# Edge scatter of a fused graph-network kernel: four one-hot buffers of four chunks in place of two, edge bias in PSUM banks of its own, first one-hots between the evictions of the values

## The reference

```python
x = x + L0_gnn(layernorm(x), batch, edges, edge_attr_16, Wq, ..., 32)   # 512 nodes, 512 wide, 8 heads
x = x + L0_ffn(layernorm(x))                                            # 8 experts, top 2
x = x + L1_gnn(layernorm(x), edges, edge_weight, ...)                   # Chebyshev, 5 terms
x = x + L1_ffn(layernorm(x))                                            # 8 experts, top 2

# L0_gnn, 32 graphs of 16 nodes
attn = einsum('bnhd,bmhd->bnmh', q, k) * scale
eb = edge_attr @ We + be                       # 16384 edges, 8 heads
attn = attn.at[src // n, src % n, dst % n].add(eb)
attn = softmax(attn, axis=2)
out = einsum('bnmh,bmhd->bnhd', attn, v)

# L1_gnn
deg = segment_sum(edge_weight, src)
norm_w = -dinv[src] * edge_weight * dinv[dst]
prop(h) = segment_sum(norm_w[:, None] * h[src], dst)
```

## Time and profile before

| | |
|---|---|
| time, median of 3 runs | 792.26 us (791.27 to 792.68) |
| time of the profiled execution | 792.48 us |
| its span | 790.7 us |
| PE, DVE, ACT busy, share of the span | 86%, 71%, 56% |
| first triple of the scatter starts, closing matmuls start | 66.96 us, 162.94 us |
| PE's granted clock, mean over the span | 0.932 |

### The profile page before, as it was taken

One profiled execution on the slowest core, in us unless ns is written; L12 is line 12 of the kernel. 1 busy time (PEld: TensorE's weight loads), 2 busy tenths in 40 slices (PEclk: granted clock), 3 DMA queues, 4 the chain that ended last, 5 costly groups with the idle time before them and its releaser, 6 DMA issues.

```text
span 790.7 us, 23111 instructions
## 1 busy us (share of the span) xinstructions
PE 676.8 (86%) x8392; PEld 569.0 (72%) x8393; DVE 563.3 (71%) x1237; ACT 444.2 (56%) x772; POOL 119.8 (15%) x175
## 2 busy tenths in 40 slices
PE   2997999957488999999993499999399999999991
PEld 1456888844378999999983244444288999999981
DVE  4665777653779888898887473435778888887881
ACT  3452666632256777787765332220367888788870
POOL 2000000010000022323214100000000234233333
PEclk9998999979679999999997699999579999999996
DMA  9500110110126889989863830000137889988864
GB/s 305 221 1 3 41 40 0 40 41 1 71 90 241 320 277 338 308 256 325 284 217 68 313 107 1 1 0 1 70 110 239 257 259 271 268 266 262 259 200 86
DMA packets 37779, 127.72 MB, mean 162 GB/s; under 512 B 5441, under 2 KB 6033, under 8 KB 37569
## 3 DMA queue, kind: packets, MB, share of 16 engines
q1 hardware_dynamic: 31712, 119.39, 43.5%
q0 software_dynamic: 3648, 6.23, 5.4%
q10 hardware_dynamic: 2352, 1.23, 0.6%
HBM read 117.85 MB, written 10.03 MB: 162 GB/s over the span
## 4 chain that ended last, share of the span: by engine, by line
PE 64%; DVE 16%; issue 7%; DMA 5%; ACT 3%; POOL 2%; ACTq 1%; DVEq 1%; SPq 0%; POOLq 0%
PE pb L1479 11%; PE pb L1480 11%; PE pb L1481 11%; PE pb L1718 6%; PE pb L1580 5%; DMA r_stage<-in_chunks 4%; PE pb L1749 3%; PE pb L1751 3%; PE pb L1750 3%; DVE r_split L950 3%; PE pb L1578 2%; PE pb L1488 2%; ACT r_split L679 2%; PE pb L1579 1%; DVE r_work L1263 1%
## 5 line engine op out<-in xcount | busy, mean ns | idle before, releaser
L950 DVE SCALAR_TENSOR_TENSOR r_split<-r_stage,r_split 128x1024 f16<-128x1024 f32 (+1 forms) x160 | 230.7, 1443 | 48.8 <-ACT r_split L679 47.1
L679 ACT ACTIVATE r_split<-r_stage 128x1024 f16<-128x1024 f32 (+1 forms) x160 | 197.2, 1236 | 49.4 <-PE pb L1751 32.3
L1479 PE MATMUL pb<-r_work,r_split 128*128 128x160 f16 x864 | 185.1, 235 | 6.8 <-DVE r_work L1339 5.1
L1480 PE MATMUL pb<-r_work,r_split 128*128 128x160 f16 x864 | 185.1, 235 | 0.0
L1481 PE MATMUL pb<-r_work,r_split 128*128 128x160 f16 x864 | 185.0, 235 | 0.0
L1749 PE MATMUL pb<-r_work,r_split 128*128 128x160 f16 x608 | 129.9, 233 | 5.4 <-DVE r_work L1327 2.8
L1751 PE MATMUL pb<-r_work,r_split 128*128 128x160 f16 x608 | 129.9, 233 | 0.0
L1750 PE MATMUL pb<-r_work,r_split 128*128 128x160 f16 x608 | 129.9, 233 | 0.0
L1578 PE MATMUL pb<-r_work 128*128 128x64 f16 x512 | 88.3, 195 | 5.2 <-DVE r_work L1075 3.0
L1479 PEld LDWEIGHTS pb<-r_work,r_split 128*128 128x128 f16 x864 | 85.3, 99 | 8.6 <-issue 6.9
L1580 PE MATMUL pb<-r_work 128*128 128x256 f16 x512 | 90.6, 277 | 0.0
(11 more groups left out here) (284 smaller groups left out, 1289.0 us busy)
## 6 DMA issues: line engine op xcount, KB each, us to landing
r_stage<-in_chunks SPq DMA_DIRECT2D x68, 768.0 KB, 4.5
r_stage<-in_chunks SPq DMA_DIRECT2D x92, 512.0 KB, 4.9
r_gnn<-in_cheb_lin SPq DMA_DIRECT2D x3, 1024.0 KB, 8.6
r_split<-in_cheb_lin SPq DMA_DIRECT2D x3, 1024.0 KB, 11.6
x_dram<-x_sb SPq DMA_DIRECT2D x10, 256.0 KB, 2.6
x_sb<-in_x SPq DMA_DIRECT2D x1, 1024.0 KB, 5.7
r_split<-in_Wq SPq DMA_DIRECT2D x1, 1024.0 KB, 9.5
r_work<-in_attr SPq DMA_DIRECT2D x1, 1024.0 KB, 11.2
```

The lines of the kernel that those rows point to most:

```text
L679: nc.scalar.activation(x.hi(c), x.stage(c), ACT.Copy, scale=W_SCALE).then_inc(x.whi, 1)
L950: V.scalar_tensor_tensor(x.lo(c), x.stage(c), W_SCALE, x.hi(c), ALU.mult, ALU.subtract)\
L1479: MM(o, sh, mh, start=start, stop=False)
L1480: MM(o, sh, ml, start=False, stop=False)
```

## The change

- **Four buffers.** In the narrow path there are four buffers (`NB` = 4) of four chunks, 7 KB a partition each (`dst` now holds 64 columns a chunk and no longer 512). DVE and ACT wait for the use of a buffer three buffers back.
- **Sources.** ACT makes one source one-hot of four in every buffer (two of eight, where it was three of eight); DVE makes the other three. ACT reads `flag_i` too, as its path now depends on it.
- **Edge bias** accumulates in `pb[6]` and `pb[7]`. PE waits for `v_ready` only before it opens the accumulations, and no longer for `score_read`. `score_m` moves to another place in SBUF.
- **Order on DVE.** One-hots of buffer 0, evictions of v 0 and 1, buffer 1, evictions 2 and 3, buffer 2, the scores, buffer 3. Within a buffer the edge-bias products now come ahead of the two weight products. `weight_lo` is done after each eight buffers, as before.
- **PE** reads `flag_i` before the v projection. Its loop body is eight rounds of two buffers (two iterations), where it was four rounds (four iterations). The closing matmuls have one column each.

The diff, cut to its core:

```diff
-        score_m = [view(r_work, 8 + b, T * H // 2 * GN, F32, "p (t h k) -> p t h k", t=T, h=H // 2) for b in range(2)]
+        score_m = [view(r_mid, 12 + b, T * H // 2 * GN, F32, "p (t h k) -> p t h k", t=T, h=H // 2) for b in range(2)]
+        NB = 4
+        src_hot_n = [view(r_work, 7 * b, GC * N, F16, "p (c n) -> p c n", c=GC) for b in range(NB)]
+        dst_n = [[view(r_work, 7 * b + 4 + 0.5 * s, GC * W, F16, "p (c n) -> p c n", c=GC) for s in range(2)]
+                 for b in range(NB)]
+        ebd_n = [view(r_work, 7 * b + 5, GC * 2 * P, F16, "p (c s q) -> p c s q", c=GC, s=2) for b in range(NB)]
...
-            def sources(i, b, free):
+            def source(b, one, hot, n):
+
+                nc.scalar.activation(src_off[:, b % 2, :], iota_n[:, :], ACT.Abs, bias=src_neg[:, one])\
+                    .then_inc(off_ready, 1)
+                act.wait_ge(off_ready, n)
+                nc.scalar.activation(hot, src_off[:, b % 2, :], ACT.Relu, bias=ones[:, 0:1], scale=-1.0)\
+                    .then_inc(hot_act, 1)
+            def sources(i, b, bufs, hot, free):
-                    act.wait_ge(hot_used, i * 2 + (b - 1))
-                if free or b > 0:
-                    act.wait_ge(hot_act, i * (2 * AC - 1) + b * AC)
-                for c in range(AC - b):
-                    one = bass.ds(i * (2 * GC) + (b * GC + c), 1)
+                    act.wait_ge(hot_used, i * bufs + (b - bufs + 1))
+                if free or b >= 2:
+                    act.wait_ge(hot_act, i * bufs + (b - 1))
+                source(b, bass.ds(i * (bufs * GC) + b * GC, 1), hot[b][:, 0, :], i * bufs + (b + 1))
...
+            narrow = act.value_load(flag_i[0:1, 0:1], min_val=0, max_val=1)
+            with act.If(narrow):
+                all_sources(NB, src_hot_n)
+            with act.Else():
+                all_sources(2, src_hot)
...
-            for t in range(T):
+            def take_scores():
-            def one_hots(i, b, free, windowed):
+            def targets(b, at, hot, ebd_b, windowed):
+
+                for c in range(1, GC):
+                    V.tensor_scalar(hot[:, c, :], iota_n[:, :], src_f[:, at(c, 1)], None, ALU.is_equal)
+                for s in range(2):
+                    last = V.tensor_tensor(ebd_b[:, :, s, :].rearrange("p c (h m two) -> p c h m two", h=H, two=2),
+                                           bc(pairs(dl_hot[:, at(0, GC), :]), 2, H),
+                                           bc(eb_2[s][:, at(0, GC), :, :], 3, GN // 2), ALU.mult)
+                return last
+
+            def near_hots(i, b, free):
+
+
+                def at(c, n):
+                    return bass.ds(i * (NB * GC) + (b * GC + c), n)
+
+                if free:
+                    dve.wait_ge(hot_used, i * NB + (b - NB + 1))
+                V.tensor_tensor(pairs(rel_hot[b % 2]),
+                                bc(iota_n[:, 0:W].rearrange("p (m two) -> p m two", two=2), 1, GC),
+                                bc(rel_2[:, at(0, GC), :], 2, W // 2), ALU.is_equal).then_inc(rel_ready, 1)
+                targets(b, at, src_hot_n[b], ebd_n[b], True)
+                dve.wait_ge(rel_ready, i * NB + (b + 1))
+                for s in range(2):
+                    last = V.tensor_tensor(pairs(dst_n[b][s]), pairs(rel_hot[b % 2]),
+                                           bc(w_2[s][:, at(0, GC), :], 2, W // 2), ALU.mult)
+                last.then_inc(hot_ready, 1)
...
-            def all_one_hots(windowed):
-                rounds = C // (2 * GC) // AHEAD
+            def all_near():
+                near_hots(0, 0, False)
+                values(0)
+                values(1)
+                near_hots(0, 1, False)
+                values(2)
+                values(3)
+                near_hots(0, 2, False)
+                take_scores()
+                near_hots(0, 3, False)
+                rounds = C // (NB * GC)
                 for c in range(AHEAD):
-                    if c == 0:
-                        one_hots(0, 0, False, windowed)
-                        one_hots(0, 1, False, windowed)
-                    with dve.Fori(max(1, rounds * c), rounds * (c + 1)) as i:
-                        one_hots(i, 0, True, windowed)
-                        one_hots(i, 1, True, windowed)
+                    with dve.Fori(max(1, rounds // AHEAD * c), rounds // AHEAD * (c + 1)) as i:
+                        for b in range(NB):
+                            near_hots(i, b, True)
                     weight_lo(ex[0], 0, c)
...
-            dve.wait_ge(score_read, 2 * T)
...
-                        pb[4 + i][:, :].rearrange("p (t s q) -> p t s q", t=2, s=2)[:, :, s, :],
+                        pb[6 + i][:, :].rearrange("p (t s q) -> p t s q", t=2, s=2)[:, :, s, :],
...
+            narrow = pe.value_load(flag_i[0:1, 0:1], min_val=0, max_val=1)
...
-            def scatter(i, b, windowed, firsts, after=None):
-                pe.wait_ge(hot_ready, i * 2 + (b + 1))
-                pe.wait_ge(hot_act, i * (2 * AC - 1) + (AC + b * (AC - 1)))
+            def scatter(i, b, bufs, c0, hot, hi, lo, ebd_b, firsts=None, after=None):
+                pe.wait_ge(hot_ready, i * bufs + (b + 1))
+                pe.wait_ge(hot_act, i * bufs + (b + 1))
...
-                        last = MM(pb[4 + t // 2][:, 256 * (t % 2):256 * (t % 2) + 256], w,
-                                  ebd[b][:, c, :, :].rearrange("p s q -> p (s q)"), start=False, stop=False,
+                        w = hot[:, c, t * P:(t + 1) * P]
+                        MM(pb[t][:, cols], w, hi[:, c, 0:n], start=False, stop=False, skip_group_check=True)
+                        MM(pb[t][:, cols], w, lo[:, c, 0:n], start=False, stop=False, skip_group_check=True)
+                        last = MM(pb[6 + t // 2][:, 256 * (t % 2):256 * (t % 2) + 256], w,
+                                  ebd_b[:, c, :, :].rearrange("p s q -> p (s q)"), start=False, stop=False,
...
-                turns = 4
+                turns = 8
                 with pe.Fori(0, C // (2 * GC * turns)) as i:
                     firsts = window_starts(i * (2 * GC * turns))
...
-                        scatter(i * turns + r, 0, True, firsts)
-                        scatter(i * turns + r, 1, True, firsts, load_next if r < turns - 1 else None)
+                        for h in range(2):
+                            b = (2 * r + h) % NB
+                            scatter(i, 2 * r + h, 2 * turns, h * GC, src_hot_n[b], dst_n[b][0], dst_n[b][1], ebd_n[b],
+                                    firsts, load_next if h == 1 and r < turns - 1 else None)
...
             pe.wait_ge(v_ready, T)
-            pe.wait_ge(score_read, 2 * T)
-            for t in range(T + 2):
-                MM(pb[t][:, :], zeros[:, :], iota_n[:, :], start=True, stop=False, skip_group_check=True)
-            narrow = pe.value_load(flag_i[0:1, 0:1], min_val=0, max_val=1)
+            totals = [pb[t] for t in range(T)] + [pb[6], pb[7]]
+            for o in totals:
+                MM(o[:, :], zeros[:, :], iota_n[:, :], start=True, stop=False, skip_group_check=True)
...
-            for t in range(T + 2):
-                last = MM(pb[t][:, :], zeros[:, :], iota_n[:, :], start=False, stop=True, skip_group_check=True)
+            for o in totals:
+                last = MM(o[:, 0:1], zeros[:, :], iota_n[:, 0:1], start=False, stop=True, skip_group_check=True)
             last.then_inc(scatter_psum, 1)
```

More of the change, by code:

```diff
@@ L133, in build_network @@
         GC = 4
-        AC = 2
         src_hot = [view(r_work, 14 * b, GC * N, F16, "p (c n) -> p c n", c=GC) for b in range(2)]
@@ L296, in build_network @@
         score_psum = sem("score_psum")
+        score_far = sem("score_far")
         score_read = sem("score_read")
@@ L706, in _ @@
                 weight_hi(ex[0], 0, c)
-            def sources(i, b, free):
-                if free:
-                    act.wait_ge(hot_used, i * 2 + (b - 1))
-                if free or b > 0:
-                    act.wait_ge(hot_act, i * (2 * AC - 1) + b * AC)
-                for c in range(AC - b):
-                    one = bass.ds(i * (2 * GC) + (b * GC + c), 1)
[L716 to L721, removed]
+            def source(b, one, hot, n):
[4 more added lines that the diff above has]
+                    .then_inc(hot_act, 1)
@@ new lines, in sources, with all_sources @@
+            def sources(i, b, bufs, hot, free):
+                if free:
+                    act.wait_ge(hot_used, i * bufs + (b - bufs + 1))
+                if free or b >= 2:
+                    act.wait_ge(hot_act, i * bufs + (b - 1))
+                source(b, bass.ds(i * (bufs * GC) + b * GC, 1), hot[b][:, 0, :], i * bufs + (b + 1))
+            def all_sources(bufs, hot):
+                for b in range(bufs):
+                    sources(0, b, bufs, hot, False)
+                with act.Fori(1, C // (bufs * GC)) as i:
+                    for b in range(bufs):
+                        sources(i, b, bufs, hot, True)
```

(52 more changed lines are left out.)

10 lines of the change are left out of this document (4 added, 6 removed).

## The result

| | before | changed |
|---|---|---|
| median, 20 runs each | 791.25 us (787.72 to 793.32) | 788.9 us (786.44 to 790.99) |
| ratio | | 0.997, 95% interval 0.9957 to 0.9984 |
| profiled execution, span, mean clock | 792.48, 790.7, 0.932 | 790.86, 788.7, 0.929 |
| scatter's first triple, closing matmuls start, end | 66.96, 162.94, 164.40 | 63.17, 158.26, 158.55 |

The forecast was 779.4 us, range 776.4 to 784.9. The direction was right and the size wrong by 10 us. The lines of the changed kernel: a triple is 1624 to 1626 (1578 to 1580 before), the opening and closing matmuls are 1661 and 1667, the experts' second products 1796 to 1798 (1749 to 1751).

What follows compares the result with a forecast made beforehand. The prediction took PE to bound the scatter, with 9.5 us of holes in 96.0. Start -4.4, length -7.6 and closing matmuls -0.9 sum to -12.9 us, from the 792.26 us median to 779.4, range 776.4 to 784.9.

Steps and rivals of the forecast that it cites:

- Length of the scatter: Scatter: PE at full clock without waits for DVE or ACT takes 88.4 us in place of 96.0, -7.6 us.
- PE's loop has one turn inside the scatter in place of three; I leave 0.5 for it: Scatter, PE's loop: the one remaining turn costs 0.5 us, for a window load less a little cover, and the branch.
- All behind the scatter waits for its result and shifts as it is: Stages behind the scatter: they move with its end unchanged, costed at nothing.
- Rival C: Behind the scatter: clock falls elsewhere, moving the end 1.6 us either way, 777.8 or 781.0; chance 0.07 beyond the forecast's own range.
- Start: Scatter's start: PE no longer waits for the score evictions; first triple at 62.55 in place of 66.96, -4.4 us.
- rival B: Scatter's start: the clock falls all the same, costing 2.2 to 3.3 us, 781.6 to 782.7; chance 0.08.
- Waits for DVE and ACT: Inside the scatter: PE's waits for both engines vanish, as four buffers let DVE be three ahead.
- rival D: Scatter: DVE becomes the bound, kernel slower above 2.97 us a buffer; chance 0.05 with any other loss ending above 794.
- Window loads: Scatter: fourteen loads of window starts in PE's sequencer cost 0.1 us each, 1.4 in all; ends 0 and 5.6.
- A0: Scatter: no window load shows, -1.4 us, 778.0 us; chance 0.15, inside the forecast's 0.62.
- A: Scatter: window loads keep their price, 0.38 each, 5.3 us in place of 1.4, 783.3 us; chance 0.14.
- Closing matmuls: Scatter's end: six matmuls of one column take 0.55 us where they took 1.46, -0.9 us (ends -0.6 and -1.2).

Runs made afterwards that it cites:

- e1: Changed kernel with PE's scatter loop back at four rounds a body: 778.01 us, ratio 0.9854 to the kernel before.
- e3: Changed kernel with all sixteen rounds in one body, so no turn: 779.0 us, ratio 0.9863 to the kernel before.
- e4: Changed kernel with two rounds a body, seven turns: 780.43 us, ratio 0.9873 to the kernel before.
- e7: Changed kernel with six rounds a body in two iterations and the last four rounds behind the loop: 777.3 us, ratio 0.985 to the kernel before.
- e2: Kernel before with only PE's loop body changed, eight rounds in place of four: 805.33 us, ratio 1.0183 to the kernel before.
- e5: Changed kernel with 64 more matmuls in the wide path, which is not taken: 785.79 us, ratio 0.9948 to the kernel before.
- e8: Changed kernel with four rounds a body and two buffers in place of four: 784.36 us, ratio 0.9926 to the kernel before.
- e6: Changed kernel with four rounds a body and 64 idle matmuls in the untaken wide path: 778.34 us, ratio 0.9844 to the kernel before.
- e10: Changed kernel with 128 more matmuls in the wide path, which is not taken: 789.14 us, ratio 0.9997 to the kernel before.
- e9: The changed kernel itself run once more, nothing altered: 788.66 us, ratio 0.9989 to the kernel before.

## Why the prediction was wrong

*The step that failed* is the sentence in "Length of the scatter": "PE's loop has one turn inside the scatter in place of three; I leave 0.5 for it". It costs 6.7 us and, by the clock, 2.2 more. The prediction took the turn for a matter of registers and a branch, and the body's double length for nothing. FETCH is shown by e1, e3, e4 and e7 against the changed kernel, and by e2 against the kernel before: with the body short, or with no turn, the kernel has 777 to 780 us, where 779.4 was forecast. The forecast stood on 792.26 us for the kernel before, which has 790 beside these runs; by the ratio it was 0.984, and they have 0.985 to 0.987.

*The second* is "All behind the scatter waits for its result and shifts as it is". The work does, but PE's code behind the scatter moved by the longer body, and two waits for it at 412 to 421 us took 4.6 us of the 5.8. e5 shows that they hang on the place alone, and e2 loses 4.1 us there with the long body alone. Rival C looked for such a loss in the clock; its mechanism was another, its size threefold.

The Trainium skill, "Runtime: NRT & Kernel Launch" (Instruction fetch mechanics), says that TensorE's instruction memory has 128 KiB, which it gives as 2048 instructions, and is refilled in 16 KiB blocks. It also says that a taken branch waits for a fetch when its target isn't in the current window of two blocks. The trace agrees in the packets' size (16 KB) and in kind: the branch back took 4.13 us. In the bound it agrees with neither figure, and the measurement decides: a body of some 1,840 instructions with its waits and loads, which is under 2048, was fetched again, and one of some 1,380 (e7), far more than two blocks of 256, was not. The page wasn't weighed in the prediction. It names the mechanism that spoke against this change, but its 128 KiB alone would have let a body of eight rounds pass.

*The other terms.*
- Start: first triple at 63.17, forecast 62.55. PE opened at 61.52, so 0.25 more than forecast for what lies ahead of it; the six opening matmuls took 1.47 where 1.3 was forecast, and the window load showed 0.18. v was ready in time, the clock stayed at 1.00: rival B is out, in place of 4.4 us the start gave 3.8.
- Waits for DVE and ACT: gone in all versions with four buffers. A buffer costs DVE 2.06 us (starts of line 1085 that follow one another), where 2.07 was read from the earlier trace rows, and DVE isn't the bound: rival D is out.
- Window loads: forecast 0.1 each. In the changed kernel, outside the stretch at half clock, no spacing but that at the turn and one (0.27 in place of 0.17) is over 0.2 us. That is A0; A is out. e8 agrees with the reading that a load shows when PE's sequencer has been held by a late buffer.
- Closing matmuls: forecast -0.9, measured -1.2 (0.29 in place of 1.46).
- Sum at the scatter's end without the hole and its half clock: 3.8 at the start, 96.0 - 86.2 = 9.8 in the length, 1.2 at the end, 14.8 us against the 12.9 of the forecast.

What stays open: where between 1,344 and 1,792 instructions the bound lies, why e2's window loads cost more, why e6's padding changed nothing, and why e10 is not the changed kernel to the tenth.

## What to carry to other kernels

A loop's unrolled body has a size that PE can hold; here 1,344 instructions were held, 1,792 were not, and one jump back cost 9 us of the 15 that all the rest had won. Before unrolling further, count the instructions of the body and look at the instruction packets: if they go on arriving while the loop runs, make the body shorter, or take the loop away. The branch's own row in the sequencer says it most directly: 0.2 us back to a body that was held, 3.8 to 6 us to one that wasn't. With a gain of a few us, look for holes far behind the edit at such a branch or just behind it, named "issue" or not: they may come and go with where the code lies, so compare versions with some idle code added before a small difference is put down to the work.

## What the runs showed that was not expected

Straight code of PE is fetched in time even at full pace (e3: 86.7 us for 512 triples, with a packet about every 6 us). Idle code in a branch that is never taken changed the time by some 3 us (e5 against e9: 0.9948 to 0.9989). And a version 12 us under the kernel before is one number away from the changed kernel: 778.0 us with four rounds a body. The 777.3 us with six can't be told from it (0.985 and 0.9854).
